# A DLRM tower on one core: other orders around the gram of the first tiles, and gram parts two by two in the middle tiles

## The reference

```python
e = jnp.stack([tbl_f[ids[:, f]] for f in range(27)], axis=1)      # 512 x 27 x 128
inter = jnp.einsum('bfd,bgd->bfg', e, e)[:, TRIU_I, TRIU_J]       # 512 x 351
h = jnp.concatenate([e.reshape(512, -1), inter, dense_ctx], axis=1)
h = jnp.maximum(h @ W_top1 + b_top1, 0.0)                         # 3823 -> 512
h = jnp.maximum(h @ W_top2 + b_top2, 0.0)                         # 512 -> 256
y = h @ W_top3                                                    # 256 -> 1
```

## Time and profile before

| | us |
|---|---|
| time before, median of 3 runs (177.14 to 177.88) | 177.21 |
| the profiled execution, its own time | 177.42 |
| its span, first to last instruction | 175.6 |
| PE busy | 150.5 (86%) |
| PEld busy | 133.7 (76%) |
| VectorE busy | 112.3 (64%) |
| GpSimd busy | 106.6 (61%) |
| ScalarE busy | 102.6 (58%) |

### The profile page before, as it was taken

One profiled execution on the slowest core, in us unless ns is written; L12 is line 12 of the kernel. 1 busy time (PEld: TensorE's weight loads), 2 busy tenths in 40 slices (PEclk: granted clock), 3 DMA queues, 4 the chain that ended last, 5 costly groups with the idle time before them and its releaser, 6 DMA issues.

```text
span 175.6 us, 2254 instructions
## 1 busy us (share of the span) xinstructions
PE 150.5 (86%) x765; PEld 133.7 (76%) x765; DVE 112.3 (64%) x205; ACT 102.6 (58%) x196; POOL 106.6 (61%) x122
## 2 busy tenths in 40 slices
PE   0135995995778997998999999999999999999894
PEld 0013794794667996897989898999898989899892
DVE  3447999998978889124675773045866753669421
ACT  2528979595489796034699363326984624484201
POOL 4777777777777777777577777775777710033000
DMA  5999999812121212121112121212112200000000
GB/s 113 305 376 370 365 374 408 233 47 64 45 62 45 60 49 61 45 60 45 45 45 63 46 60 45 57 48 49 45 49 59 54 24 0 0 0 0 4 0 0
DMA packets 9443, 16.75 MB, mean 95 GB/s; under 512 B 3604, under 2 KB 4120, under 8 KB 9304
## 3 DMA queue, kind: packets, MB, share of 16 engines
q1 hardware_dynamic: 5976, 9.53, 16.3%
q0 software_dynamic: 3456, 7.08, 14.5%
HBM read 16.61 MB, written 0.00 MB: 95 GB/s over the span
## 4 chain that ended last, share of the span: by engine, by line
PE 56%; ACT 12%; DVE 10%; DMA 9%; issue 6%; POOL 6%; ACTq 0%; DVEq 0%
PE h_ps L573 10%; PE h_ps L574 9%; PE h_ps L575 9%; DMA rows<-in_tbl,ids_sb 8%; POOL rows L244 6%; PE gram_ps L602 5%; ACT stage_a L304 5%; PE tp_ps L552 5%; PE gram_ps L676 3%; DVE y L419 3%; PE h_ps L617 3%; PE h_ps L619 3%; PE h_ps L618 3%; ACT y L294 2%; DVE stage_a L427 2%
## 5 line engine op out<-in xcount | busy, mean ns | idle before, releaser
L244 POOL DMA_INDIRECT rows<-in_tbl,ids_sb x108 | 102.7, 951 | 36.8 <-issue 27.7
L573 PE MATMUL h_ps<-w_hi,e 128*128 128x512 f32 x108 | 53.4, 494 | 0.6 <-DVE e L407 0.6
L407 DVE TENSOR_TENSOR e<-tp_ps,e 128x512 fp32r<-128x512 f32 (+1 forms) x28 | 32.0, 1158 | 21.9 <-ACT e L276 21.4
L574 PE MATMUL h_ps<-w_lo,e 128*128 128x512 f32 x108 | 44.1, 408 | 0.0
L575 PE MATMUL h_ps<-w_hi,e 128*128 128x512 f32 x108 | 43.7, 404 | 0.0
L276 ACT ACTIVATE e<-tp_ps 128x512 fp32r<-128x512 f32 (+1 forms) x28 | 28.9, 1055 | 16.1 <-PE tp_ps L552 12.9
L552 PE MATMUL tp_ps<-ident,rows 128*128 128x128 f32 x108 | 22.3, 294 | 17.0 <-DMA rows<-in_tbl,ids_sb 16.1
L573 PEld LDWEIGHTS h_ps<-w_hi,e 128*128 128x128 f32 x108 | 32.9, 304 | 2.5 <-DVE e L407 0.9
L574 PEld LDWEIGHTS h_ps<-w_lo,e 128*128 128x128 f32 x108 | 33.9, 314 | 0.0
L575 PEld LDWEIGHTS h_ps<-w_hi,e 128*128 128x128 f32 x108 | 33.0, 305 | 0.4
L552 PEld LDWEIGHTS tp_ps<-ident,rows 128*128 128x128 f32 x108 | 14.0, 145 | 23.2 <-DMA rows<-in_tbl,ids_sb 10.3
(11 more groups left out here) (67 smaller groups left out, 133.4 us busy)
## 6 DMA issues: line engine op xcount, KB each, us to landing
stage_a<-in_W_top SPq DMA_DIRECT2D x10, 512.0 KB, 5.9
w_pairs<-in_W_pairs SPq DMA_DIRECT2D x1, 1792.0 KB, 9.3
rows<-in_tbl,ids_sb POOLq DMA_INDIRECT x108, 2.6
y<-in_W_top SPq DMA_DIRECT2D x3, 512.0 KB, 10.7
w<-in_W_top SPq DMA_DIRECT2D x1, 512.0 KB
y<-in_W_top SPq DMA_DIRECT2D x1, 256.0 KB, 4.1
out_y<-stage_a SPq DMA_DIRECT2D x4, 0.5 KB
ids_sb<-in_ids SPq DMA_DIRECT2D x1, 40.5 KB, 3.8
```

The source lines that it names most:

```text
L244: nc.gpsimd.indirect_dma_start(rows[:, n % RING, :], None, tables[f], bass.IndirectOffsetOnAxis(ids_sb[:, t, f:f + 1], 0)).then_inc(rows_l ...
L407: nc.vector.tensor_tensor(features(1, fs[0], fs[-1] + 1), tp_ps[k % 2][:, 0:len(fs), :], features(0, fs[0], fs[-1] + 1), ALU.subtract).the ...
L573: nc.tensor.matmul(out, hi, w_hi[:, f, :], start=f == 0, stop=False)
L574: nc.tensor.matmul(out, hi, w_lo[:, f, :], start=False, stop=False)
```

## The change

Nothing that is computed changes, only orders and one wait.

- Tile 0, ScalarE and VectorE: the split of quad 6 comes before the split of the last weight chunk (ScalarE) or of the last two (VectorE). ScalarE's first half copy also waits for its own 27th w split.
- Tile 0, TensorE: the E steps run eight features behind the transposes instead of six, and the two held back run between gram parts, which changes the places of the others there.
- Tile 0, moves: the moves of the first half stand behind the whole gram, one in front of the split of tile 1's quad 1 and one behind it, no longer between the sums.
- Tile 1: two E steps run before quad 5's transposes, not after them, and two behind the h1 transposes.
- VectorE's order of sums, splits and moves (2 and 3 for 0 and 1) changes in the same way as ScalarE's, whose diff stands below; in tiles 2 and 3 its `copy_y(u - 1)` stays behind `split_e(t, 1)`.
- Middle tiles: gram parts and E steps come two and two (from 1 E step between parts to 2 between pairs), transposes of the next quad 0 stand before part 4, one of the two early moves stays within the gram, behind sum 5, and the other is behind `relu_h2`.

```diff
                 if part == 0 and t == 0:
                     act.wait_ge(w_lo_ready, F - 2)
+                    act.wait_ge(w_hi_ready, F)
...
-            for q in range(NQ):
+            for q in range(NQ - 1):
                 for c in quad_features(q):
                     split_w(c)
                 split_e(0, q)
+            split_w(F - 3)
+            split_w(F - 2)
+            split_e(0, NQ - 1)
+            split_w(F - 1)
             for t in range(1, NT):
                 u = t - 1
                 sums(u, 0, 2)
                 split_ctx(u)
-                sums(u, 2, 5)
-                move_x(u, 0, 0)
-                sums(u, 5, 6)
-                move_x(u, 0, 1)
-                sums(u, 6, GP)
-                split_e(t, 0)
-                if u >= 1:
+                if t == 1:
+                    sums(u, 2, GP)
+                    split_e(t, 0)
+                    move_x(u, 0, 0)
+                    split_e(t, 1)
+                    move_x(u, 0, 1)
+                else:
+                    sums(u, 2, 6)
+                    move_x(u, 0, 0)
+                    sums(u, 6, GP)
+                    split_e(t, 0)
                     relu_h2(u - 1)
-                split_e(t, 1)
+                    move_x(u, 0, 1)
+                    split_e(t, 1)
                 move_x(u, 1, 0)
                 split_e(t, 2)
                 move_x(u, 1, 1)
...
             def grams(t):
                 gram(t, 0)
                 gram(t, 1)
-                embeddings_h1(t, 20, 21)
+                embeddings_h1(t, 20, 22)
                 gram(t, 2)
-                embeddings_h1(t, 21, 22)
                 gram(t, 3)
-                embeddings_h1(t, 22, 23)
+                embeddings_h1(t, 22, 24)
+                transposes(t + 1, 0)
                 gram(t, 4)
-                embeddings_h1(t, 23, 24)
-                transposes(t + 1, 0)
                 gram(t, 5)
-                embeddings_h1(t, 24, 25)
+                embeddings_h1(t, 24, 26)
                 gram(t, 6)
-                embeddings_h1(t, 25, 26)
                 gram(t, 7)
                 embeddings_h1(t, 26, 27)
 
             for f in range(F):
                 transpose(0, f)
-                if f >= 6:
-                    embeddings_h1(0, f - 6, f - 5)
+                if f >= 8:
+                    embeddings_h1(0, f - 8, f - 7)
...
                     gram(u, 0)
                     gram(u, 1)
+                    embeddings_h1(u, 19, 20)
+                    gram(u, 2)
+                    embeddings_h1(u, 20, 21)
+                    gram(u, 3)
                     embeddings_h1(u, 21, 22)
-                    gram(u, 2)
-                    gram(u, 3)
-                    embeddings_h1(u, 22, 23)
                     gram(u, 4)
                     transposes(t, 0)
                     gram(u, 5)
+                    embeddings_h1(u, 22, 23)
+                    gram(u, 6)
                     embeddings_h1(u, 23, 24)
-                    gram(u, 6)
                     gram(u, 7)
                     transposes(t, 1)
                     embeddings_h1(u, 24, 27)
...
                 embeddings_h1(t, 8, 12)
...
                 if t == 1:
-                    embeddings_h1(t, 13, 16)
+                    embeddings_h1(t, 12, 14)
+                    transposes(t, 5)
+                    embeddings_h1(t, 14, 16)
                     pairs_h1(u)
                     transposes(t, 6)
-                    embeddings_h1(t, 16, 20)
+                    embeddings_h1(t, 16, 18)
                     transpose_h1(u)
+                    embeddings_h1(t, 18, 20)
```

More of the change, by code:

```diff
@@ L490, in _ @@
                     nc.vector.memset(x_full, 0.0).then_inc(x_zeroed, 1)
[L491 to L497, removed]
+                if t == 1:
+                    sums(u, 2, GP)
+                    split_e(t, 0)
+                    move_x(u, 0, 2)
+                    split_e(t, 1)
+                    move_x(u, 0, 3)
+                else:
+                    sums(u, 2, 6)
+                    move_x(u, 0, 2)
+                    sums(u, 6, GP)
+                    split_e(t, 0)
                     relu_h2(u - 1)
-                split_e(t, 1)
-                if u >= 1:
+                    move_x(u, 0, 3)
+                    split_e(t, 1)
                     copy_y(u - 1)
@@ L738, in _ @@
                 embeddings_h1(t, 8, 12)
[L739 to L744, removed]
                 if t == 1:
-                    embeddings_h1(t, 13, 16)
+                    embeddings_h1(t, 12, 14)
+                    transposes(t, 5)
+                    embeddings_h1(t, 14, 16)
                     pairs_h1(u)
                     transposes(t, 6)
-                    embeddings_h1(t, 16, 20)
+                    embeddings_h1(t, 16, 18)
                     transpose_h1(u)
-                elif t < NT - 1:
+                    embeddings_h1(t, 18, 20)
+                else:
+                    pairs_h1(u, 0, 3)
+                    transposes(t, 5)
+                    pairs_h1(u, 3)
+                    embeddings_h1(t, 12, 13)
+                if 1 < t < NT - 1:
                     embeddings_h1(t, 13, 16)
```

## The result

The changed kernel took 174.72 us in the median of 4 runs (173.88 to 176.28), the kernel before 177.18 (177.14 to 177.88): a ratio of 0.985, 95% interval 0.981 to 0.989. It is faster, by 2.5 us where 3.3 were forecast. The profiled execution took 174.12 us for a span of 172.3, that is 3.3 us under the profiled one of before. Its runs are spread over 2.4 us, those of before over 0.7; that was not forecast. Ratios and their intervals, here and in the experiments, compare fast runs only, while medians and ranges take in all runs; on chip I of the experiments the kernel before took 177.4 to 178.2 us in seven executions and 182.1 to 184.2 in seven slow ones.

The account below looks back on a forecast made before the run. TensorE's own instructions bound it from 68 us, gathers one each 1.25 us before; 1.92 + 0.73 + 0.74 = 3.4 us off profiled 177.42 gives 174.0, off median 177.21 gives 173.8; taken 173.9, range 173.2 to 175.4.

Parts of the forecast that it names:

- signs of being wrong: Feature 23 after 68.5, TensorE waiting for split or x part after 66, 0.43 us matmuls after 42, layer 2 over 10.6 late.
- rival B: Tile 1: moves ahead of splits 1 to 3 make E step 12 late 1 us beyond its cover; 174.8; chance 0.08.
- Row gates: Tile 1: gathered rows 46 and 50 land near 63.0 and 68.0 regardless of other engines, taking back tile 0's 2.4 us.
- first gate: Row 46, last of tile 1's quad 4: TensorE would be there at 61.2 and gets it at 63.0, 1.8 us cover.
- Part 1: Tile 0's end: earlier quad 6 split starts the gram 0.91 us earlier, at 41.97; tile 1's quad 2 2.4 us ahead.
- Part 2: Tile 1: E steps 12, 13 ahead of quad 5 give -1.41, covered h1T copy -0.56; gram at 78.5, 1.92 us in sum.
- second gate: Row 50, feature 23 of tile 1, lands near 68.0; its 1.01 us TensorE wait was to be filled by E steps.
- Part 3: Middle tiles' gram stages: fewer runs of E steps and fewer waits, -0.73 and -0.74 us, to 10.17 and 9.93.
- Rival A: Middle tiles: pairs bring own waits, ScalarE's queue behind move_x 0.3 us or more later; 175.3; chance 0.12.
- covers of 0.24 to 0.56 us: Middle tiles: thin time margins of 0.24, 0.45 and 0.56 us, each relative to TensorE's own pace.
- Rival C: TensorE's clock falls ahead of tile 0's gram; slower only if over 6.1 us are lost, about 179; chance 0.03 (or any loss).
- The pause of GpSimd: Gather queue near 87 us: the 1.79 us pause goes away; tightest later row, 73, lands 1.0 us early.

Follow-up runs that it names:

- tile 0's part alone: Kernel before with only the tile 0 edits (split order, lag of eight, moves behind the gram): 177.27 us on chip I, ratio 0.9965.
- lag of six: Changed kernel with tile 0's E steps again six features behind the transposes, 19 and 20 not between gram parts: 175.22 us on chip I, ratio 0.985 to before.

## Why the prediction was right, point by point

The size of the total is in part luck. In the profiled pair 3.3 us came off for 3.4 summed up, but tile 1's part brought 0.68 less than forecast, the middle gram stages 0.35 more, and 0.2 came from elsewhere. Two of the prediction's own signs of being wrong appeared: TensorE waited for a split after 66 us, and feature 23 was transposed near 68.8, later than 68.5. And the median of 174.72 is within 0.1 us of rival B's 174.8; that B was there only in part is read from the stretches, not from the total.

**Row gates.** Right, and shown by tile 0's part alone. The first gate was worth less cover than worked out (0.44 us of wait, not 1.8), since tile 0 came 1.2 to 1.5 us later than in the sum.

**Part 1, tile 0's end.** The step from the last transpose to the gram went as worked out: 43.18 - 40.92 = 2.26 us, where before it was 42.88 - 39.67 = 3.21, so 0.95 gained for 0.91. From the gram to quad 2 it was 11.99 us for 13.28, and 11.73 forecast. What failed is its starting point, a context transpose that ends at 39.94. I took it over from one execution; in this one row 16 came 0.56 us later and the clock fell near 31 us. At the first gate the price stayed hidden. But the sentence "tile 0 may go 1.8 us worse than worked out and it costs nothing" was wrong: the sum itself gave split 3, which hangs on tile 0's end through ScalarE's and VectorE's queues, a cover of only 0.9 us. That one gave way first.

**Part 2, the second gate.** -1.92 forecast, -1.24 measured. The wait at feature 23 was filled and the h1T copy covered (TensorE goes on from E step 19 into the gram without idle time). Most of the missing 0.7 us are in the term "E step 12 needs split 3 at 66.3: 0.9 us to spare". It was wanted at 66.5 and split 3 ended at 66.9. VectorE's timeline:

```profile
62.16 1.29 DVE L437 COPY stage_a<-y 27x112 f32<-27x112 f32 x4
64.10 1.23 DVE L444 TENSOR_TENSOR x<-stage_a,x 128x384 fp32r<-128x384 f32 x3 [0.65 <-ACT x L317]
65.71 1.18 DVE L417 TENSOR_TENSOR e<-tp_ps,e 128x512 fp32r<-128x512 f32 x1 [0.38 <-ACT e L276]
```

The last move ends at 63.45 for 62.0 worked out, and split 3 is late by the same 1.5 us, tile 0's delay. 1.5 less the cover of 0.9 leaves 0.6 us. The chain of waits of the changed kernel runs through these instructions into E step 12, and not through a gather:

```profile
59.85 1.08 ACT e L276
...
62.92 0.27 DVE stage_a L437
...
63.98 0.71 ACT x L317 x2
64.69 1.00 ACT e L276
...
65.71 1.19 DVE e L417
...
66.95 0.61 PE h_ps L587
```

An estimate from TensorE's rows agrees. Without the wait quad 5 would have started at 67.7, and feature 23 would have met row 50, which landed near 68.2 (gather 50 at 65.78 for 65.43, 2.4 us to landing); it was transposed near 68.8. That is 0.6 us for split 3 and some 0.15 for the later row. So rival B's mechanism was there at about half its size: 0.48 us of idle time here, 0.71 in the lag of six, for 1 us. That the order of the moves, rather than the delay alone, holds split 3 back is argued from the queue (the x splits stand in front of it); the run meant to test it said nothing.

**Part 3, two and two.** -0.73 and -0.74 forecast, -1.03 and -0.79 measured. Rival A did not come: with full occupation of TensorE in both stages none of the covers of 0.24 to 0.56 us gave way. What was off is tile 1's start: I kept 1.13 us for its first gram pair, which was slow only because it came after a wait. Without the wait, and with E steps ahead of it, the pair takes 0.89 (the chain of waits of the changed kernel, with the first matmul of the run behind it):

```profile
79.35 0.89 PE gram_ps L616 x8
80.24 0.35 PE h_ps L587
80.59 0.24 PE h_ps L588
```

That is 0.24 of the 0.30 us by which tile 1's stage beat the forecast. The first matmul of a run still costs 0.35 us, so the price per change of operation is real, and the trace goes against reading the Trainium skill (TensorE: Matmul & The Clock Gate, Step-by-step) as if pulling weight loads ahead made it nothing.

**Rival C, the clock.** The fall came, but near 31 us, in front of the gates and not before the gram, and three profiles with different orders have it. It cost about 0.7 us of tile 0's 1.25 and at most 0.7 at tile 1's gram, far from the 6.1 us at which it would have decided. The 1.8 us that the rival allowed before any loss were too many, since split 3's 0.9 came first. The Trainium skill (TensorE: Matmul & The Clock Gate, Part 1) says of the clock's rise, after which matmuls come faster, that its moment varies from run to run. The traces agree: with the same lag on TensorE the matmuls became fast near 21.7 us in the profile of before and near 20.5 in the lag of six, near 24.7 in the changed kernel and 23.2 in tile 0's part alone. The fall varied too: it stayed away after a wait of 1.79 us in the profile of before and came after 1.31, 2.31 and 1.96 in the three others.

**The pause of GpSimd** went as forecast, and row 73 was the tightest. The sum counted its 1.0 us of margin as safe; the lag of six shows that one long gather is enough to pass it, and half of all traces have one.

**The size.** Of the median's 177.2 - 174.7 = 2.5 us, against 3.3 in the profiled pair, 0.8 us is scatter that the forecast did not have. A long gather is a cause that was seen at work (1.1 us, once). That it is the cause of the two runs of the changed kernel at 175.3 and 176.3 is not shown, since they have no trace.

One sentence of the change's description was wrong: VectorE split quad 6 ahead of chunks 25 and 26 before the change too (L481 to L484). Only ScalarE's order of it was changed. The sum had it right, as VectorE's queue was taken from its rows.

**What stays open:** how the 2.5 us divide between tile 1's order and the middle tiles other than by stretches of traces in which both are present, and whether a kernel without tile 0's part or with split 3 first would be faster still.

## What to carry to other kernels

A stage that runs ahead of a paced stream (here a gather each 1.25 us) gains nothing from being faster; the gain is in what can be moved in front of the point where it waits for the stream. Before summing up a change, find the first row behind the edit that comes at its own time, and test by making only the edits ahead of it. A stretch can have several covers, and the smallest of them holds: here 1.8 us at the gate counted for nothing beside 0.9 at a split in another queue. And when an edit takes the last pauses out of a queue, as here out of GpSimd's, its margin for a slow instruction goes with them: look at the spread of the runs, not at the median alone.

## What the runs showed of the hardware that was not expected

- One gather instruction on GpSimd took 4.08 and 4.45 us in two of the four readable traces, at number 52 and 51, for a median of 0.94; in the two others the longest was 1.28. Five of the ten traces of the disturbed chips have one too, 4.11 to 4.51 us, at number 53 or 54.
- TensorE's granted clock fell to 0.50 near 31 us in three of the four readable traces, with waits of 1.31, 2.31 and 1.96 us before it, and not after 1.79 us in the fourth.
- On chips II and III the kernel before took 18 to 20% longer. In the traces from there ScalarE stood idle before the splits of its quads for 13 to 30 us in total with no releaser in the program, up to 11 us at once.
